# Cross-attention and feed-forward with FP4 rounding: the residual of six groups, the scale bounds and the reciprocals move between VectorE, ScalarE and Pool

## The reference

```python
scale = max(max(abs(block)) / 6, 1e-12)
q = nearest value of {0, 0.5, 1, 1.5, 2, 3, 4, 6} to abs(block) / scale
result = q * sign(block) * scale
gate, up = linear(x, w_gate), linear(x, w_up)
h = silu(gate) * up
out = linear(h, w_down)
```

## Time and profile before

| | |
|---|---|
| median of 3 runs | 220.07 us (219.77 to 220.28) |
| the profiled execution | 220.49 us, of which its span is 218.6 us |
| mean granted clock of TensorE | 0.982 of full speed |
| feed-forward part | about 127 us to the end |

### The profile page before, as it was taken

How to read it: one execution, slowest core, us unless ns; L and a number is a source line. 1 busy time by engine, 2 the same in 40 slices (tenths; PEclk the granted TensorE clock), 3 DMA queues, 4 the chain that set the end, 5 groups by cost and what they waited for, 6 DMA issues and landing times.

```text
span 218.6 us, 5689 instructions
## 1 busy us (share of the span) xinstructions
PE 185.7 (85%) x2045; PEld 140.4 (64%) x2045; DVE 174.5 (80%) x391; ACT 132.3 (61%) x264; POOL 139.1 (64%) x203
## 2 busy tenths in 40 slices
PE   0739979979999999998998996577599999999963
PEld 0218665966959669496686773355377878878753
DVE  6418784998798976769768899996599999999941
ACT  2362797957877878788768733452446556665441
POOL 6272655388978681854818575898539776667750
PEclk9997999999999999999999999999799999999999
DMA  6989650220200000000000000000010110101111
GB/s 199 260 252 373 232 171 24 70 80 3 99 0 4 3 0 3 4 0 3 0 4 3 4 0 0 0 0 1 1 51 0 48 48 3 48 1 51 48 49 49
DMA packets 13665, 11.97 MB, mean 55 GB/s; under 512 B 766, under 2 KB 10558, under 8 KB 13630
## 3 DMA queue, kind: packets, MB, share of 16 engines
q1 hardware_dynamic: 13078, 11.29, 16.5%
q10 hardware_dynamic: 560, 0.33, 0.5%
HBM read 9.52 MB, written 2.10 MB: 53 GB/s over the span
## 4 chain that ended last, share of the span: by engine, by line
PE 43%; POOL 15%; issue 8%; DVE 6%; ACT 5%; POOLq 0%; ACTq 0%; DVEq 0%
PE bank L967 7%; PE bank L943 6%; PE bank L946 6%; PE bank L887 4%; POOL hq L372 3%; POOL wq_y L357 3%; PE bank L955 3%; PE bank L896 3%; PE bank L897 2%; PE bank L875 2%; ACT xn L409 2%; POOL xn L254 2%; PE a_pair L838 2%; PE bank L838 2%; ACT val L421 2%
## 5 line engine op out<-in xcount | busy, mean ns | idle before, releaser
L967 PE MATMUL bank<-wdT,hT 128*128 128x128 f32 x192 | 27.4, 280 | 4.3 <-ACT hT L543 3.3
L943 PE MATMUL bank<-guT,xqT 128*128 128x352 f32 x64 | 25.2, 477 | 4.4 <-DVE hh L730 4.4
L372 POOL TENSOR_TENSOR hq<-wq_u,sch 128x704 f32<-128x704 f32 x16 | 22.2, 1386 | 10.1 <-DVE wq_u L757 10.0
L967 PEld LDWEIGHTS bank<-wdT,hT 128*128 128x128 f32 x192 | 24.3, 194 | 5.3 <-ACT hT L543 3.5
L946 PE MATMUL bank<-guT,xqT 128*128 128x352 f32 x64 | 24.9, 471 | 1.5 <-ACT mask_bc L475 1.5
L357 POOL TENSOR_TENSOR wq_y<-hh,ivh 128x704 f32<-128x704 f32 x16 | 22.5, 1406 | 3.7 <-DVE ivh L745 3.3
L475 ACT ACTIVATE mask_bc<-bank 128x352 f32<-128x352 f32 x32 | 14.6, 459 | 14.0 <-PE bank L943 13.6
L543 ACT COPY hT<-bank 128x384 f32<-128x384 f32 x32 | 15.3, 478 | 12.6 <-PE bank L955 12.6
L875 PE MATMUL bank<-cT,wsT 128*128 128x512 f32 x32 | 16.6, 647 | 6.2 <-DMA cT<-in_ctxT 6.2
L610 DVE TENSOR_REDUCE den<-prob 128x8 f32<-128x512 f32 x32 | 19.8, 666 | 0.0
L887 PE MATMUL bank<-wsT,cT 128*128 128x128 f32 x128 | 19.0, 297 | 0.6 <-DVE q_m L595 0.6
(11 more groups left out here) (117 smaller groups left out, 482.5 us busy)
## 6 DMA issues: line engine op xcount, KB each, us to landing
cT<-in_ctxT SPq DMA_DIRECT2D x8, 512.0 KB, 5.1
x_all<-in_x SPq DMA_DIRECT2D x8, 256.0 KB, 5.5
mask_bc<-in_mask_rows SPq DMA_DIRECT2D x8, 256.0 KB, 6.1
out_y<-mask_bc SPq DMA_DIRECT2D x8, 256.0 KB, 2.2
wsT<-in_WsT ACTq DMA_DIRECT2D x1, 256.0 KB, 3.9
w_all<-in_wg SPq DMA_DIRECT2D x1, 176.0 KB
w_all<-in_wu SPq DMA_DIRECT2D x1, 176.0 KB
w_all<-in_wd SPq DMA_DIRECT2D x1, 176.0 KB
```

The source lines that it names most:

```text
L372: nc.gpsimd.tensor_tensor(hq[i][:, :, 0:I].rearrange("p t (n k) -> p t n k", k=BLK), rh[i][:, :, :].rearrange("p (t n) k -> p t n k", t=2) ...
L943: nc.tensor.matmul(gu_bank[2 * n % 3][:, 0:I], xqT[g % 2][:, t], guT[:, 0, :], start=True, stop=True).then_inc(pe_g, 1)
L967: last = nc.tensor.matmul(d_bank[:, j * P:(j + 1) * P], hT[n % 2][:, c, :], wdT[:, c, :], start=(c == 0), stop=(c == 2))
```

## The change

- The bounds uph of a unit are computed by Pool (h_bounds) and not by VectorE, into two buffers in turn. In Pool's loop they come first in iteration u, ahead of hq_unit(u - 2); they wait for h_max(u).
- VectorE's h_reciprocal(u) is the reciprocal alone. It moves from iteration m = 2u + 1, behind h_max(u), to m = 2u + 2, behind the product of that iteration and ahead of h_round(u - 1).
- The residual of groups 0 to 5 is split: ScalarE copies d_bank to y_out (down_evac, at the start of m = 12, 16, ... 32, ahead of silu), and Pool adds x_all to it in place (residual_sum(g), behind y_unit in u = 5, 7, ... 15). Groups 6 and 7 stay on VectorE.
- down(4g) waits for ScalarE's copy of the group before it, for g to 6, and for VectorE's residual for g = 7. The store's semaphore becomes one for each group.

```diff
+            def h_bounds(u):
+                pool.wait_ge(amh_ok, u + 1)
+                past(pool, ivh_ok, u - 1)
+                nc.gpsimd.tensor_scalar(uph[u % 2][:, :], amh[u % 2][:, :], SIXTH_UP, TINY_UP,
+                                        ALU.mult, ALU.max).then_inc(uph_ok, 1)
...
+            def residual_sum(g):
+                pool.wait_ge(d_ok, g + 1)
+                ys = y_out[g % 2][:, :, :]
+                nc.gpsimd.tensor_tensor(ys, ys, x_all[:, tiles(g), :], ALU.add).then_inc(yo_ok[g], 1)
+
             for u in range(UNITS + 2):
+                if u < UNITS:
+                    h_bounds(u)
                 if 0 <= u - 2:
                     hq_unit(u - 2)
                 if u == 3:
@@
                 if u < UNITS:
                     h_scales(u)
                     y_unit(u)
+                if u % 2 and on((u - 5) // 2) and u < UNITS + 1:
+                    residual_sum((u - 5) // 2)
...
+            def down_evac(g):
+                act.wait_ge(pe_dn, (g + 1) * TILES)
+                past(act, out_d[g % 2], 16 * (g // 2))
+                nc.scalar.copy(y_out[g % 2][:, :, :].rearrange("p t d -> p (t d)"), d_bank[:, :]).then_inc(d_ok, 1)
+
             for m in range(NT + LAG + 1):
+                if m <= NT and (m - LAG - 1) % TILES == 0 and on((m - LAG - 1) // TILES - 1):
+                    down_evac((m - LAG - 1) // TILES - 1)
                 if m < NT:
                     silu(m)
...
             def h_reciprocal(u):
-                dve.wait_ge(amh_ok, u + 1)
-                past(dve, ivh_ok, u)
-                nc.vector.tensor_scalar(uph[:, :], amh[u % 2][:, :], SIXTH_UP, TINY_UP, ALU.mult, ALU.max).then_inc(uph_ok, 1)
                 dve.wait_ge(uph_ok, u + 1)
                 past(dve, yh_ok, u - 1)
-                nc.vector.reciprocal(ivh[u % 2][:, :], uph[:, :]).then_inc(ivh_ok, 1)
+                nc.vector.reciprocal(ivh[u % 2][:, :], uph[u % 2][:, :]).then_inc(ivh_ok, 1)
...
             for m in range(NT + LAG + 2):
                 if m < NT:
                     h_product(m)
-                if m < NT and (m - LAG) % TILES == 0 and on((m - LAG) // TILES - 1):
-                    residual((m - LAG) // TILES - 1)
+                if m % 2 == 0 and 0 <= m // 2 - 1 < UNITS:
+                    h_reciprocal(m // 2 - 1)
                 if m == 0:
                     s3_round(NG - 3)
                 if m % 2 == 0 and 0 <= m // 2 - 2 < UNITS:
                     h_round(m // 2 - 2)
                 if m % 2 and m < NT:
                     h_max(m // 2)
-                    h_reciprocal(m // 2)
...
                 if j == 0:
-                    past(pe, yo_ok, g)
+                    past(pe, d_ok, min(g, DOWN_BY_ACT))
+                    if g > DOWN_BY_ACT:
+                        pe.wait_ge(yo_ok[g - 1], 1)
```

More of the change, by code:

```diff
@@ L30 @@
 LAG = 7
+DOWN_BY_ACT = 6
 EPS = 1e-5
@@ L115, in xattn_ffn @@
         amh = [sb(f"amh{i}", [P, 2 * NB_H]) for i in range(2)]
-        uph = sb("uph", [P, 2 * NB_H])
+        uph = [sb(f"uph{i}", [P, 2 * NB_H]) for i in range(2)]
         ivh = [sb(f"ivh{i}", [P, 2 * NB_H]) for i in range(2)]
@@ L160, in xattn_ffn @@
             sem(n) for n in ("pe_x0", "x0_ok", "pe_t", "t_ok", "pe_g", "pe_u", "pe_dn"))
-        sg_ok, h_ok, amh_ok, uph_ok, ivh_ok, sch_ok, yh_ok, ah_ok, uh_ok, rh_ok, hq_ok, yo_ok = (
+        sg_ok, h_ok, amh_ok, uph_ok, ivh_ok, sch_ok, yh_ok, ah_ok, uh_ok, rh_ok, hq_ok, d_ok = (
             sem(n) for n in ("sg_ok", "h_ok", "amh_ok", "uph_ok", "ivh_ok", "sch_ok", "yh_ok", "ah_ok",
-                             "uh_ok", "rh_ok", "hq_ok", "yo_ok"))
+                             "uh_ok", "rh_ok", "hq_ok", "d_ok"))
+        yo_ok = [sem(f"yo_ok{g}") for g in range(NG)]
         x_tiles = x.rearrange("(n p) d -> p n d", p=P)
@@ L193, in store @@
             def store(g):
-                sp.wait_ge(yo_ok, g + 1)
+                sp.wait_ge(yo_ok[g], 1)
                 sp.dma_start(out_tiles[:, tiles(g), :], y_out[g % 2][:, :, :]).then_inc(out_d[g % 2], 16)
@@ L764, in residual @@
                 nc.vector.tensor_tensor(y_out[g % 2][:, :, :], d_bank[:, :].rearrange("p (t d) -> p t d", t=TILES),
-                                        x_all[:, tiles(g), :], ALU.add).then_inc(yo_ok, 1)
+                                        x_all[:, tiles(g), :], ALU.add).then_inc(yo_ok[g], 1)
             for m in range(NT + LAG + 2):
```

## The result

| | before | changed |
|---|---|---|
| median | 220.18 us (4 runs) | 226.90 us (4 runs, 225.85 to 227.53) |
| ratio to before | | 1.0305, 95% interval 1.0265 to 1.0344 |
| profiled execution, span | 220.49, 218.6 | 226.42, 224.6 |

Slower by 6.7 us, where 4.2 had been forecast. The median lies on the upper end of the predicted range (221.4 to 226.9), and two of the four runs, 227.38 and 227.53, lie above it: that the range holds is in part luck. The two profiled spans differ by 6.0. I cut the feed-forward part of each trace at three marks: the first product of out_project (127.29 before, 127.07 after), down(3), and the end of gate_up(31), which is the start of its up product plus 0.59, the time from the start of one such product to the next.

What follows compares the result with a forecast made beforehand. Pool bounds the first stage, a never-waiting PE the second, a chain through Pool the last. First stage +2.64, steady stage 0, last +1.53 sum to +4.17 us: predicted median 224.2, range 221.4 to 226.9.

Steps and rivals of the forecast that it cites:

- (a) to (e): First stage, link by link: delays from bounds and reciprocal, from y(2) to the y of group 7, in sum +2.64 us.
- The same loss again, net 0: PE's low clock around down(3): 1.7 us lost as in the kernel before, so no net change.
- the case put at +1.7: PE's low clock around down(3) lasting twice as long: 1.7 us more.
- The steady stage: cost 0: Middle stretch, down(3) to gate_up(31): Pool's 8.66 us per four tiles fits under PE's 9.18, so no time is lost.
- The cover, put at 0.6: Steady stage: time between the end of hq and PE's transpose of it, shrinking from 2.4 to about 0.6 us, unbroken.
- The copy covers it: Steady stage: down(4g+4) comes 1.5 us behind down(3+4g), so its wait for ScalarE's copy of d_bank costs nothing.
- waits of PE for hq: Steady stage: the named sign that its cost would not be 0.
- Pool is now the bound: Last stage, from y(14) on: Pool's work sets the pace and hq(14) starts 1.53 us later.
- the bound of 1.30: Pool's residual sum: upper limit of its duration in us, against 1.06 taken; 0.24 more per sum.
- (3): Rival, worse: sums at 1.30, the 0.6 cover broken at some transposes, or longer low clock; 226.1 us, 17%.
- (1): Rival, faster: VectorE's relief reaches the end, as Pool finds the maxima ready for its bounds; 218.2 us, 9%.
- my 1.5: Residual sum: Pool taken as 1.5 times slower than VectorE, 1.06 against 0.69 us.

Runs made afterwards that it cites:

- e4: Kernel before with only the bounds on Pool, ahead of hq, and the reciprocal moved; residual stays on VectorE: 226.63 us.
- e3: Kernel before with only the residual split (ScalarE's copy, Pool's sum); bounds and reciprocal stay on VectorE: 220.35 us.
- e1: Changed kernel with Pool's bounds(u) moved from ahead of hq(u-2) to behind it, just ahead of the scales of u: 224.22 us.
- e2: Changed kernel with ScalarE's copy of d_bank moved ahead of the magnitudes, to the end of the iteration before: 226.51 us.
- e7: e4 with ScalarE's magnitudes of unit u moved from the end of iteration 2u+3 to behind silu(2u+4): 225.69 us.
- e5: e1 with Pool's sum(5) moved from ahead of hq(14) to behind it: 222.87 us.
- e6: e3 with Pool's sum(5) moved behind hq(14): 219.17 us, ratio to the kernel before 0.9945.
- e8: Changed kernel, Pool's sum in groups 1, 3, 4, 5 given other operands or multiplication; one execution: plain sum 1.27 us, broadcast or same operands 1.04 to 1.07.
- e11: Changed kernel, Pool's sum in groups 1, 2, 3 given different or same operands, in or out of place; one execution: 1.27 us different, 1.04 to 1.07 same.
- e9: e6 with the rounding of group 7 moved later (ScalarE's magnitudes, VectorE's rounding, Pool's xq): 217.04 us, 0.984 of before.

## Why the prediction was right, and where it failed

**First stage: right.** The links (a) to (e) can be laid beside the trace, each time corrected by the 0.22 us by which this execution came earlier: y(2) +0.40 (predicted +0.51), hq(1) +1.07 (+1.01), the wait of the fourth bounds 1.36 (1.33), hq(2) +2.79 (+2.70), end of the y of group 7 +2.73 (+2.64). e4 shows that the bounds and the reciprocal make it, e3 that the residual has no part in it, e1 that half of it is the order on Pool alone. "The same loss again, net 0" for the low clock was not quite right: the clock stayed low about twice as long (0.51 from 156 to 163 us, against 0.76), the case put at +1.7, but PE stood still for the first 2.2 us of it, and it cost 0.57 in the middle.

**"The steady stage: cost 0": this step failed.** It counted each engine's work against PE's 9.18 us, and one cover, that of hq before its transpose; both held, and PE never idled for hq in this stretch. The cover, put at 0.6, was 0.20 to 1.58 for units 4 to 12. It left out a second thing that the order moves. y(u) goes behind hq(u-2) as well, and ScalarE, in order, waits for y with its magnitudes, in front of silu and the copy of d_bank. "The copy covers it" looked at the 1.5 us between the two downs and not at what stands ahead of the copy in ScalarE's queue. Measured: 1.08 us of PE's waits, which e2 takes away, and e1 but for 0.25, and 0.57 of low clock. That silu is held up by the same waits, e4 and e7 show. I had named "waits of PE for hq" as the sign of this failure; the sign was PE's wait for ScalarE. In e4, which has no copy, it was the named sign after all.

**The last stage: the size nearly right, the reason half wrong.** +1.91 against +1.53. I had said "Pool is now the bound" from y(14) on. But Pool still waited 0.33 us for h_max(15). The sum comes out from h_max(15): it ends 0.74 earlier after gate_up(31) than before (1.96 us behind it, not 2.70), then 1.68 more to y(15), 1.23 for sum(5) ahead of hq(14), and 0.28 less, since hq(14) no longer waits for its rounding: +1.89. The sum, taken at 1.06, measured 1.27, near the bound of 1.30; that is 0.2 of the 0.4. By e5 and e6 sum(5) in front of hq(14) costs 0.9.

**Of the rivals,** (3), which named 226.1 and a sum at 1.30, lay nearest to the time, by sums and low clock; its broken cover at the transposes didn't occur in the middle of the changed kernel, but did in e4. The largest piece beyond the forecast, PE's 1.0 us of waits for ScalarE, is in no rival, so that 226.1 comes so near is in part chance. (1) has its core of truth in the last stage: with the sum out of the way, VectorE's relief does reach the end (e6).

What stays open: of the 6.7 us by the medians, the profiles place 6.0. Runs of the changed kernel spread from 225.85 to 227.53, with spans of 224.0 at a mean clock of 0.983 and 225.7 at 0.962; why the clock differs from run to run no experiment here tells. How the two halves, 0.1 and 6.3 us alone, share the middle and last stage when both are made isn't separated further. Nor is the bounds' move to Pool separated from the reciprocal's later place on VectorE: of e1's remaining 3.9 us no run tells which of them costs it.

## What to carry to other kernels

Where an instruction is put ahead of others in an in-order queue, follow each of the others that it delays to its readers, and there look at what stands behind the reader in its queue: in the middle stretch 1.1 us was lost two queues on, on ScalarE, with Pool busy 41 of 49 us. A wait placed ahead of ready work costs more than its instruction: bounds of 0.36 us cost 1.36 of waiting where their input depended on the same engine. Relief of an engine can be undone by the work that takes its place, where that stands in front of the last chain: with sum(5) one place later the last stretch was 0.9 us shorter.

## What the runs showed of the hardware

- Pool's element-by-element instruction of 128x512 float32 takes 1.27 us with two different full operands and 1.04 to 1.07 with one of them broadcast or both the same (e8, e11). The six sums of the changed kernel took 1.26 to 1.28, also beside VectorE's product and rounding, which have one input in PSUM. VectorE took 0.69 for the same sum with one operand in PSUM, so the ratio is 1.85 for this sum, nearer to the twofold that the Trainium skill gives (GPSIMD Engine Reference, Key points) than my 1.5.
- Pool was slowed beside VectorE's rounding of group 7, whose operands are both in SBUF: bounds 0.73 instead of 0.36 and hq 1.67 instead of 1.39, while VectorE kept its 0.68 and 0.69. In the kernel before VectorE's second step took 1.75 and Pool's y(5) 1.70; both came again in e9 (161.21 and 160.72 us). The Trainium skill (GPSIMD Engine Reference, Specifications) names this contention. In these traces the longer one was each time the one that started second: y(5) at 159.37 behind VectorE's first step (first line below, from the kernel before), the second step at 159.87 behind y(5), and in the changed kernel Pool's bounds and hq (last two lines). But VectorE's second step at 160.63, which started while the bounds ran, was no longer than elsewhere: no rule is shown.

```profile
159.20 0.63 DVE L645 SCALAR_TENSOR_TENSOR u<-a,y 128x512 f32<-128x512 f32 x1
159.92 0.68 DVE L669 SCALAR_TENSOR_TENSOR u<-a,y 128x512 f32<-128x512 f32 x1
160.63 0.69 DVE L673 SCALAR_TENSOR_TENSOR r<-a,u 128x512 f32<-128x512 f32 x1
160.09 0.73 POOL L366 TENSOR_SCALAR uph<-amh 128x44 f32<-128x44 f32 x1 [2.96 <-DVE amh L760]
160.90 1.67 POOL L380 TENSOR_TENSOR hq<-wq_u,sch 128x704 f32<-128x704 f32 x1
```
